# The layer norm behind each attention chunk, done at once from PSUM instead of one chunk later from a copy, and two sets of PSUM copies moved from ScalarE to VectorE

## The reference

```python
x = x + LN(attn(LN(x), Wq, Wk, Wv, Wo))         # causal, one head of width 1024
x = x + LN(ffn(LN(x), qweights, scales, ...))   # three blocks of two quantised linear layers with LoRA,
                                                # each with layer norm and gelu between, and a residual
```

## Time and profile before

| | us |
|---|---|
| median of 3 runs | 5109.56 (5102.74 to 5114.68) |
| the profiled execution, slowest core | 5117.42 |
| its span on core 3, from the first to the last instruction | 5115.9 |
| spans of all 8 cores | 5087.0 to 5115.9 |
| PE busy | 2732.4 (53%) |
| ACT busy | 1645.8 (32%) |
| DVE busy | 1080.8 (21%) |
| POOL busy | 217.7 (4%) |
| chain that ended last | PE 42%, ACT 20%, issue 14%, DVE 13%, DMA 9% |

### The profile page before, as it was taken

How to read it: one execution, slowest core, us unless ns; L and a number is a source line. 1 busy time by engine, 2 the same in 40 slices (tenths; PEclk the granted TensorE clock), 3 DMA queues, 4 the chain that set the end, 5 groups by cost and what they waited for, 6 DMA issues and landing times.

```text
span 5115.9 us, 39306 instructions; the slowest of 8 cores (5087.0 to 5115.9 us)
## 1 busy us (share of the span) xinstructions
PE 2732.4 (53%) x12112; PEld 1134.6 (22%) x12112; DVE 1080.8 (21%) x2064; ACT 1645.8 (32%) x3151; POOL 217.7 (4%) x404
## 2 busy tenths in 40 slices
PE   1248765445565577732221565656465665557564
PEld 0013322222232333311100122212121222222121
DVE  1110000211111111122220322223222322222322
ACT  4432222333323322232220433333333433433333
POOL 0000111001010111100000000000000000000000
PEclk9999997667677788865555777768676777768676
DMA  1111212222332333322210001010101001010100
GB/s 55 54 58 45 90 47 92 78 74 75 89 96 79 91 98 99 95 65 75 75 47 22 21 9 46 13 54 13 45 21 45 20 5 50 13 54 13 46 21 29
DMA packets 129701, 270.18 MB, mean 53 GB/s; under 512 B 29718, under 2 KB 70934, under 8 KB 129500
## 3 DMA queue, kind: packets, MB, share of 16 engines
q1 hardware_dynamic: 74460, 137.62, 9.4%
q0 software_dynamic: 32000, 104.88, 6.6%
q10 hardware_dynamic: 23040, 25.18, 1.4%
HBM read 208.89 MB, written 58.72 MB: 52 GB/s over the span
## 4 chain that ended last, share of the span: by engine, by line
PE 42%; ACT 20%; issue 14%; DVE 13%; DMA 9%; ACTq 1%; SPq 1%; DVEq 1%; POOLq 0%; POOL 0%
PE PB L855 7%; PE PB L433 5%; PE PB L394 5%; PE PB L785 3%; DVE stp L119 3%; PE PB L495 3%; ACT L134 3%; ACT sqd L121 3%; DVE zbuf L805 2%; ACT gT L832 2%; PE PB L231 2%; PE PB L827 2%; PE PB L649 2%; ACT wT L655 2%; PE PB L839 2%
## 5 line engine op out<-in xcount | busy, mean ns | idle before, releaser
L785 PE MATMUL PB<-wT,hTb 128*128 128x512 bf16 x1536 | 447.9, 444 | 144.7 <-DVE zbuf L811 125.2
L855 PE MATMUL PB<-gT,wT 128*128 128x512 bf16 x1536 | 388.0, 398 | 22.1 <-ACT raT L844 22.1
L827 PE MATMUL PB<-ident,g_sb 128*128 128x128 bf16 x768 | 118.5, 294 | 465.6 <-ACT g_sb L818 327.6
L394 PE MATMUL PB<-qbuf,kT 128*128 128x256 bf16 x2176 | 304.7, 288 | 29.5 <-DMA qbuf<-qTs 29.5
L872 DVE TENSOR_TENSOR hTf<-PB,hTf 128x512 f32<-128x512 f32 x192 | 132.8, 692 | 799.1 <-PE PB L867 795.0
L433 PE MATMUL PB<-vbuf,expT 128*128 128x512 bf16 x1088 | 283.9, 384 | 0.5 <-DMA vbuf<-vs 0.5
L121 ACT ACTIVATE sqd<-PB 128x1024 bf16<-128x1024 f32 x128 | 129.8, 1014 | 450.1 <-DVE stp L119 282.5
L394 PEld LDWEIGHTS PB<-qbuf,kT 128*128 128x128 bf16 x2176 | 223.7, 103 | 117.1 <-issue 30.1
L785 PEld LDWEIGHTS PB<-wT,hTb 128*128 128x128 bf16 x1536 | 151.0, 108 | 427.3 <-issue 325.4
L649 PE MATMUL PB<-ident,dqb 128*128 128x128 bf16 x384 | 101.6, 265 | 268.1 <-ACT wT L655 168.6
L403 ACT ACTIVATE expT<-PB 128x256 bf16<-128x256 f32 x272 | 104.3, 384 | 406.6 <-PE PB L394 405.9
(11 more groups left out here) (104 smaller groups left out, 3687.1 us busy)
## 6 DMA issues: line engine op xcount, KB each, us to landing
vbuf<-vs POOLq DMA_DIRECT2D x272, 256.0 KB, 3.1
qwt<-qw SPq DMA_DIRECT2D x48, 512.0 KB, 3.6
xtile<-x SPq DMA_DIRECT2D x32, 512.0 KB, 3.6
x_res<-x SPq DMA_DIRECT2D x32, 512.0 KB, 5.0
x2s<-x_sb ACTq DMA_DIRECT2D x32, 512.0 KB, 5.2
x2res<-x2s SPq DMA_DIRECT2D x32, 512.0 KB, 3.9
out<-x2res POOLq DMA_DIRECT2D x32, 512.0 KB, 2.9
gmb<-gm SPq DMA_DIRECT2D x24, 512.0 KB, 4.7
```

Of the source, the lines that this page charges most:

```text
L394: qsl=qsl: e.matmul(pa, kT[:, m * S + tt * 128: m * S + (tt + 1) * 128], qbuf[:, qsl * NJ * 256 + m * 256: qsl * NJ * 256 + (m + 1) * 256] ...
L785: pY=pY: e.matmul(pY[:, oc * 512:(oc + 1) * 512], hTb[:, j * 512 + ssi * 128: j * 512 + (ssi + 1) * 128], wT[:, l1 * NJ * 1024 + j * 1024 ...
L827: ttr = emit("t", lambda e, j=j, ssi=ssi: e.transpose(pTc[:, ssi * 128:(ssi + 1) * 128], g_sb[:, ssi * 1024 + j * 128: ssi * 1024 + (j + 1 ...
L855: tmm = emit("t", lambda e, j=j, oo=oo, l2=l2, zsl=zsl: e.matmul(pZ[:, zsl * 512:(zsl + 1) * 512], wT[:, l2 * NJ * 1024 + j * 1024 + oo * 128:
```

## The change

The tail is no longer a function that is called a chunk late. It stands in the loop, right behind the projection, and works on the same chunk. `lnsrc` and its two copies (L508) are gone: the statistics and the norm of the attention output read `pAV0` and `pAV1` in PSUM. The accumulators are released for the next chunk by the norm and no longer by the copy. The call behind the loop is gone too, and the first chunk has a tail of its own.

Three kinds of copies out of PSUM go from ACT to DVE: `rs_col` (128x2, one per chunk), `attnT` (128x256 bf16, eight per chunk) and `xnT_st` (the same shape, eight per chunk). The stores that follow the last kind stay on ACT's stream. The `snap` lines are marks for shortened builds and emit nothing.

```diff
-                lnsrc = EB(nc.sbuf_tensor("lnsrc", [128, 4 * 1024], F32))
...
-                    tec = emit("s", lambda e: e.copy(out=rs_col[:], in_=pTrs[:, 0:2]),
+                    tec = emit("v", lambda e: e.tensor_copy(out=rs_col[:],
+                                                            in_=pTrs[:, 0:2]),
                                (ttr0, ttr1))
...
-                        tev = emit("s", lambda e, j=j: e.copy(
+                        tev = emit("v", lambda e, j=j: e.tensor_copy(
                             out=attnT[:, j * 256:(j + 1) * 256], in_=pTb[:, 0:256]),
                             (tt0, tt1))
...
-                    tcps = []
                     for ss in range(2):
-                        lsl = 2 * (c % 2) + ss
-                        la_ = lnsrc[:, lsl * 1024:(lsl + 1) * 1024]
-                        tcp = emit("s", lambda e, ss=ss, la_=la_: e.copy(
-                            out=la_, in_=pAVs[ss][:]),
-                            (tproj[ss], lnsrc_rd[lsl]))
-                        pAV_rd[ss] = tcp
-                        tcps.append((tcp, la_, lsl))
-
-                    def epilogue_tail(c, tcps):
...
-                            m_ap, rs_ap, nm_ap, tm, trs_, tnm, reg, tsq = ln_stats(
-                                la_, 1024, (tcp,))
...
+                        m_ap, rs_ap, nm_ap, tm, trs_, tnm, reg, tsq = ln_stats(
+                            pAVs[ss][:], 1024, (tproj[ss],))
...
+                        tap = emit("s", lambda e, ss=ss, rs_ap=rs_ap, nm_ap=nm_ap:
+                                   e.activation(out=lnb[:], in_=pAVs[ss][:],
+                                                func=AF.Identity, scale=rs_ap,
+                                                bias=nm_ap),
+                                   (tnm, lnb_rd), strict=(trs_,))
+                        reg(tap)
+                        pAV_rd[ss] = tap
...
-                            tev = emit("s", lambda e, dst=dst: e.copy(
-                                out=dst, in_=pTb[:, 0:256]),
-                                (tt0, tt1, xst_rd[stsl] if j == 0 else None))
...
+                        tev = emit("v", lambda e, dst=dst: e.tensor_copy(
+                            out=dst, in_=pTb[:, 0:256]),
+                                   (tt0, tt1, xst_rd[stsl] if j == 0 else None))
...
-                    if pending_tail is not None:
-                        epilogue_tail(pending_tail[0], pending_tail[1])
-                    pending_tail = (c, tcps)
                     snap2l.append({e: len(ops[e]) for e in STREAMS})
-                epilogue_tail(pending_tail[0], pending_tail[1])
```

More of the change, by code:

```diff
@@ L350, in build @@
                 attn_rd = [A_done, A_done]
-                attnT_rd = [A_done]
+                attnT_rd = A_done
                 xres_rd = [A_done, A_done]
                 x2_rd = [A_done, A_done]
-                lnsrc_rd = [A_done] * 4
                 x2sp_rd = [None, None]
@@ L357, in build @@
                 xst_rd = [A_done, A_done]
-                lnb_rd = [A_done]
+                lnb_rd = A_done
                 vb_ctr = [0]
-                pending_tail = None
                 snap2l = []
@@ L475, in build @@
                             attn_sb[:, 0 * 1024 + j * 128: 0 * 1024 + (j + 1) * 128],
-                            ident[:]), (attn_rd[0], attnT_rd[0]))
+                            ident[:]), (attn_rd[0], attnT_rd))
                         tt1 = emit("t", lambda e, j=j: e.transpose(
@@ L484, in build @@
                         at_evs.append(tev)
-                        attnT_rd[0] = tev
+                        attnT_rd = tev
                     attn_rd[0] = at_evs[-1]
@@ L582, in build @@
-                    if pending_tail is not None:
-                        epilogue_tail(pending_tail[0], pending_tail[1])
-                    pending_tail = (c, tcps)
+                        row0 = s0 + ss * 128
+                        xsl = ss
+                        xa = x_res[:, xsl * 1024:(xsl + 1) * 1024]
+                        tlx = emit("q", lambda e, row0=row0, xa=xa: e.dma_start(
+                            out=xa, in_=x_h[row0:row0 + 128, :]),
+                            (xres_rd[xsl],), dmach="xr%d" % xsl)
@@ new lines, in build @@
+                        if c == 0 and ss == 0:
+                            snap40 = {e: len(ops[e]) for e in STREAMS}
+                        m_ap, rs_ap, nm_ap, tm, trs_, tnm, reg, tsq = ln_stats(
+                            pAVs[ss][:], 1024, (tproj[ss],))
+                        if c == 0 and ss == 0:
+                            snap41 = {e: len(ops[e]) for e in STREAMS}
+                        tap = emit("s", lambda e, ss=ss, rs_ap=rs_ap, nm_ap=nm_ap:
[3 more added lines that the diff above has]
+                                   (tnm, lnb_rd), strict=(trs_,))
@@ new lines, in build @@
+                        reg(tap)
+                        pAV_rd[ss] = tap
+                        if c == 0 and ss == 0:
+                            snap42 = {e: len(ops[e]) for e in STREAMS}
+                        x2a = x2_sb[:, ss * 1024:(ss + 1) * 1024]
+                        tx2 = emit("v", lambda e, x2a=x2a, xa=xa: e.tensor_add(
+                            out=x2a, in0=lnb[:], in1=xa),
+                            (tap, tlx, x2_rd[ss], x2sp_rd[ss]))
+                        lnb_rd = tx2
@@ new lines, in build @@
+                        xres_rd[xsl] = tx2
+                        if c == 0 and ss == 0:
+                            snap43 = {e: len(ops[e]) for e in STREAMS}
+                        tspx2 = emit("s", lambda e, row0=row0, x2a=x2a: e.dma_start(
+                            out=x2s[row0:row0 + 128, :], in_=x2a), (tx2,),
+                            dmach="sd%d" % ss)
+                        x2_spill_toks.append(tspx2)
+                        x2sp_rd[ss] = tspx2
+                        if c == 0 and ss == 0:
+                            snap44 = {e: len(ops[e]) for e in STREAMS}
@@ new lines, in build @@
+                        m2_ap, rs2_ap, nm2_ap, tm2, trs2, tnm2, reg2, _ = ln_stats(
+                            x2a, 1024, (tx2,))
+                        if c == 0 and ss == 0:
+                            snap45 = {e: len(ops[e]) for e in STREAMS}
+                        xna = x2n_sb[:, ss * 1024:(ss + 1) * 1024]
+                        txn = emit("v", lambda e, x2a=x2a, xna=xna, m2_ap=m2_ap,
+                                   rs2_ap=rs2_ap: e.tensor_scalar(
+                            out=xna, in0=x2a, scalar1=m2_ap, scalar2=rs2_ap,
+                            op0=ALU.subtract, op1=ALU.mult),
+                            (x2n_rd[ss],), strict=(tm2, trs2))
@@ new lines, in build @@
+                        reg2(txn)
+                        x2_rd[ss] = txn
+                        if c == 0 and ss == 0:
+                            snap46 = {e: len(ops[e]) for e in STREAMS}
+                        x2n_rd[ss] = None
+                    if c == 0:
+                        snap35 = {e: len(ops[e]) for e in STREAMS}
+                    stsl = c % 2
+                    for j in range(NJ):
+                        tt0 = emit("t", lambda e, j=j: e.transpose(
+                            pTb[:, 0:128],
+                            x2n_sb[:, 0 * 1024 + j * 128: 0 * 1024 + (j + 1) * 128],
+                            ident[:]), (x2_rd[0], attnT_rd))
+                        tt1 = emit("t", lambda e, j=j: e.transpose(
+                            pTb[:, 128:256],
+                            x2n_sb[:, 1 * 1024 + j * 128: 1 * 1024 + (j + 1) * 128],
+                            ident[:]), (x2_rd[1],))
+                        dst = xnT_st[:, stsl * NJ * 256 + j * 256: stsl * NJ * 256 + (j + 1) * 256]
+                        tev = emit("v", lambda e, dst=dst: e.tensor_copy(
+                            out=dst, in_=pTb[:, 0:256]),
+                                   (tt0, tt1, xst_rd[stsl] if j == 0 else None))
+                        attnT_rd = tev
+                        tsp = emit("s", lambda e, j=j, s0=s0, dst=dst: e.dma_start(
+                            out=hTs[j * 128:(j + 1) * 128, s0:s0 + 256], in_=dst),
+                            (tev,), dmach="hs%d" % stsl)
+                        hT_spill_toks.append(tsp)
+                        if j == NJ - 1:
+                            xst_rd[stsl] = tsp
+                            x2n_rd[0] = tev
+                            x2n_rd[1] = tev
```

## The result

The changed kernel takes 5047.5 us (median of 8 runs) against 5107.1 us for the kernel before (median of 8): the ratio is 0.9879, interval 0.9868 to 0.9890. The ratio leaves out executions in which one half of the chip ran at a lower granted clock than the other, here one of the changed kernel's eight, at 5134.9 us. Forecast were 5043 us, in a range of 5025 to 5084, and faster. The medians lie 59.6 us apart. Of the 66.8 us in the sum, stage B gave 61.6: from the reciprocal of chunk 0 to the instruction that opens stage C it was 2273.37 - 843.95 = 1429.4 us before, and is 2211.45 - 843.67 = 1367.8 us now.

The account below looks back on a forecast made before the run. The bound was each tail's exposed ACT and DVE chain, with PE waiting before the transposes. Terms 48.3 + 2.6 + 19.2 - 3.3 = 66.8 us took the profiled 5117.4 to 5050.6, less 7.9 for the median: 5043, range 5025 to 5084.

Parts of the forecast that it names:

- (1): Tail start: squares of half 0 begin 3.02 us earlier per chunk, before the projection ends; 48.3 us saved.
- (2): Tail's squares and norm read PSUM instead of lnsrc: 0.16 us a chunk, 2.6 us saved.
- (6): Chunk 0's own tail: a table load there and a cold start of chunk 1's scores; 3.3 us lost.
- (3): Small copies in the transpose rounds on DVE at 0.292 us: 0.080 saved each, 19.2 us for 240.
- A: Rival: DVE copies from PSUM at one element per step, 0.43 us; sum 33.7, time 5076; chance 0.25.
- (4): The rs_col copy on DVE, 16 times: costed at nothing, within 1.6 us in all.
- (5): Stores to hTs stay on ACT, no longer between its copies in the rounds: counted as nothing.
- (7): Loads of x and queries keep their order, accumulators are released later but before PE needs them; no cost counted.
- the 28 us: Sign: time from projection to next scores, at chunk 0's end too; 28.1 us forecast, from 31.84.
- B: Rival: head start unused, as row sum waits for whole projection or its second half runs at 1.2 GHz; 5098; chance 0.05.
- C: Rival: the 240 DVE copies eat all other gains; at 692 ns each 29 us slower, 5139; chance 0.04.
- D: Rival: no change, 5110, an unseen wait giving back what is gained; chance 0.04.

Follow-up runs that it names:

- e4: The kernel before with only the tail called for its own chunk, not a chunk late; lnsrc and the copies on ACT stay; ratio to before 1.0003.
- e5: The kernel before, tail still late but cut into 22 steps between the next chunk's scores tiles, small copies on DVE; 4725.5 us, ratio to before 0.9189.
- e3: The changed kernel, but half 0's first row sum waits for the whole projection; ratio to before 0.9978.
- e2: The changed kernel with the three kinds of small copies back on ACT; ratio to before 0.9897.
- e1: The kernel before with only the three kinds of small copies moved to DVE, tail still late and reading lnsrc; ratio to before 0.9982.

## Why the prediction was right

- **What bounds the kernel.** Shown. The chain of the tail lay in the open behind each projection, and e4 and e5 show both sides of it: where it stands in the streams decides, and not whether its data are a chunk old.
- **The sum.** It said 66.8 us; the medians fell by 59.6 and stage B by 61.6. The time came closer than that, 4.5 us off, because the sum was taken from a median of three runs, 5109.6, and the median of eight is 5107.1.
- **(1) The head start.** Forecast 48.3 us: 3.45 us per chunk for the start on half 0, 55.2 in all, less the row sum that it brings into the open. e3 took the start away and lost 54.0. The start itself came 2.04 us ahead of the projection's end, for 2.02.
- **(2) PSUM in place of `lnsrc`.** Squares 1.015 and norm 1.203 us, as in the rows of stage C. With (1) and (6) the sum gives 47.6, and e2 shows 46.5.
- **(3) The copies.** Two elements per step, 292 ns; A (one per step, 0.43) is refuted by the row. The 240 copies were put at 19.2 us; stage B of e1 is 17.3 shorter, 16.2 of it in the pieces with the rounds. The term was a little too large: a round fell from 0.985 to 0.913 us, so by 0.072 and not by 0.080. The gap between PE's last transpose and the copy is 0.01 us longer on DVE than on ACT. The Trainium skill ("VectorE: DVE Perf Modes", the perf-mode tier table) allows twice the basic rate for a 16-bit copy out of PSUM, and the trace agrees. The cycle table of the same page ("The TRN2 errata") gives an estimate of 0.26 us, and 0.292 was measured.
- **(4), (5), (7).** Nothing was seen of them. The copy of `rs_col` takes 160 ns on either engine, and PE waits for no load of x or queries within the chunks.
- **(6) Chunk 0's tail.** The start of chunk 1 cost 3.81 - 1.85 = 1.96 us more, the figure forecast; over its whole scores loop it is 9.50 against 7.47 us. The Trainium skill ("ScalarE: Activation LUTs", "What ACT_TABLE_LOAD costs") adds a drain of about 1.4 us to each load; no run here shows it, and in e5 the root starts at 1789.13, 0.02 us after its load has ended.
- **What was missed.** The scores loops of chunks 2 to 15 take 567.2 us in all where before they took 564.6. The pieces ahead of the projections gave 8.3 us of the 10.2 that (3) has for them. These 2.6 and 1.9 us are most of the 5 by which the sum is above stage B. The loops take 566.6 us in e1 and in e3, which have the copies on DVE, but 563.6 in e2 and 564.7 in e4, which have them on ACT. So it comes with the copies, and the clock goes with it: in the changed kernel, e1 and e3 PE was at 1.2 GHz for 62.9 to 65.4 us of these loops, and before, in e2 and in e4 for 56.1 to 59.3. As a mean over all eight cores the changed kernel's loops are 1.3 us longer than before and have 4.8 us more at 1.2 GHz, so the size is less certain than the direction. Why shorter rounds leave more of the following scores at 1.2 GHz is not shown.
- **The signs.** The squares, the rounds, the copies and the 28 us came as announced. One sign did not quite come: no wait of PE in front of the first transposes was to be above 10 us, and the longest were 10.2 (L558) and 11.8 (L562). The prediction's own sum leaves about 10 and nearly all of the second.

Of the rivals, the first form of B was made real by e3 and cost what it said, and the second did not occur, as no projection took longer than 9.9 us, where it needed 13; C would have needed a copy of 0.57 us; D had no wait to show.

## What to carry to other kernels

When engines work off their streams in order, ask of a piece of work not when its data are ready but what stands in front of it and behind it. Deferring it by a whole iteration and then writing it at the same place hid next to nothing here (e4); cut up and written into the gaps of the next loop, the same work took 6.4% off the changed kernel (4725.5 against 5047.5 us). Where it has to stay in the open, let it begin on the first half of what it needs.

## What the runs showed of the hardware

- A square root between exponentials costs ACT two table loads of 1.28 us. In chunk 15 of e5 PE lost nothing of the first root, since its scores loop leaves ACT idle for 1.66 us per tile and PE runs one tile ahead; behind the second it waited 0.44 us for the norm.
- DVE reads bf16 from PSUM at two elements per step: 292 ns for 256 columns, against 372 ns on ACT.
- Where the holes were filled, PE's clock was higher: a granted 0.94 in e5 over the stretch to chunk 15's reciprocal, 0.81 in the changed kernel.
- PE's clock also moves pieces that an edit doesn't touch: the same 16 projections took 147.2 us with 69.7 of them at 1.2 GHz (before) and 144.1 with 63.4 (e1), so half a microsecond for each at the lower level.
